# Summing expert answers in DRAM by accumulating scatters instead of storing them apart and adding them later

## The chip, the cores and the metric

The kernel runs on one core of one Trainium2 chip. The metric is the device time in microseconds. The kernel before has a median of 1523.21 us over 3 runs (1523.09 to 1526.4). The profiled execution took 1526.19 us, of which the profile shows a span of 1524.4 us from the first to the last instruction.

## What is computed

The input is four images of 256 channels and 64 x 64 pixels. A first layer (group norm, a 3 x 3 neighbourhood attention, a residual sum) and the attention of a second layer (a gated mean over a window of 64 tokens) come first. Then each of the 16384 tokens, a row of 256 numbers, goes through a mixture of experts:

```python
logits = tokens @ router_w.T
probs = softmax(logits)                    # 8 experts
rw, re = top_k(probs, 2)
rw = rw / maximum(rw.sum(-1), 1e-12)       # two weights that add up to 1
combine = zeros((N, E)).at[arange(N)[:, None], re].set(rw)
out = tokens
for e in range(8):
    h = gelu(tokens @ w1[e] + b1[e]); y = h @ w2[e] + b2[e]
    out = out + combine[:, e:e + 1] * y
x = from_tokens(t + out)                   # back to channels first
```

Only the two chosen experts of a token have a weight that is not zero, so a token needs two answers: 2 x 16384 answers in all.

## The kernel before

Three loops follow one another, each ended by a barrier of all engines.

**Loop 1** runs over 32 blocks of 512 tokens. Besides the first layer and the attention it normalizes each token (tile `tn`), finds the logits and sorts the tokens by expert. Each of a token's two copies goes to the next free row of its expert in the DRAM tensor `sent`, by indirect DMAs of GpSimd (128 rows each, eight for a block, line 1492). A row has 258 numbers: 256 of the token, the row in `answers` where the first copy's answer belongs, and the first expert's number. The residual row of each token, `tt`, is stored in DRAM as `residual`. `power` on GpSimd (line 1484) finds the reciprocal roots of the norms, ahead of the sends. Behind the last block VectorE builds the tables that say which tile belongs to which expert, splits the weights of the experts into two parts for exact products (`lower_parts`), and computes the two weights of every token (`mix`, lines 1450 to 1468) out of the kept logits, with one exponential on ScalarE.

**Loop 2** runs over 72 tiles of 512 sorted rows; 64 would do if every expert's count were a multiple of 512, and the rest are tiles of padding. It is a pipeline in which every engine runs an order that is written out by hand, with stages a fixed number of iterations apart (`LAG`): L loads a tile of rows (`xin`, SyncE), X turns it on TensorE and splits it (`xh` on ScalarE, `xl` on VectorE), H is the first product with its gelu (`hid`, `hh` on ScalarE, `hl` on VectorE), Y is the second product, whose bias VectorE adds into `yy` (line 1770). `yy` has three slots (`YB`). GpSimd then sends the tile's rows to `answers`, each to a place of its own, in four indirect DMAs of 128 rows of 1 KB (line 1627). They wait for `yy` and for the row numbers (`dest_i`), and not for earlier scatters. VectorE waits for a scatter only when it wants to fill the slot that this scatter read, three tiles later.

**Loop 3** runs over 32 blocks of 512 tokens: SyncE loads the two answers of each token (`got`, 1 MB) and the residual (`res`, 0.5 MB); VectorE multiplies and adds (lines 1827 and 1835); TensorE turns the sum to channels first (line 1850); ScalarE copies it out of PSUM (`fin`, two slots) and stores it (0.5 MB).

Of the kernel before, what the change touches and what calls it, by code (L numbers as in the profile page):

```python
# [88 lines left out]
def hybrid(nc, x, wqT, wkT, wvT, wo, bq, bk, bv, bo, wpT, bp, wg, rwT, w1, b1, w2, b2, out):  # L89
    f32 = mybir.dt.float32  # L90
    f32r = mybir.dt.float32r
    bf16 = mybir.dt.bfloat16
    i32 = mybir.dt.int32
# [27 lines left out]
    NJ = 2 * NT // BT + E  # L121
    NJ += NJ % 2
# [7 lines left out]
    with ctx:  # L130
# [9 lines left out]
        residual_v = nc.dram_tensor("residual", [NB, P, KT * C], f32).ap()  # L140

        sent = nc.dram_tensor("sent", [ROOM, C + 2], f32).ap()

        blanks = nc.dram_tensor("blanks", [E * BT, C + 2], f32).ap()

        answers = nc.dram_tensor("answers", [2 * NT + 2 * (E + SPARE) * BT, C], f32).ap()
# [8 lines left out]
        halves = sb("halves", [P, 2, 4])  # L155
        expert_ids = sb("expert_ids", [P, E])
# [35 lines left out]
        tail_id = sb("tail_id", [P, E + SPARE, KT, 2])  # L192
        mix = sb("mix", [P, NB * KT, 2])
# [110 lines left out]
        with nc.Block() as block:  # L304
# [20 lines left out]
            def _(eng):  # L325
# [9 lines left out]
                eng.wait_ge(pool_const, done)  # L335
                eng.memset(ones[:, :], 1.0).then_inc(pool_const, 1)
# [12 lines left out]
                eng.iota(places[:, :], pattern=[[2 * BT, NB], [2, KT]], base=0, channel_multiplier=2 * KT,  # L349
# [69 lines left out]
            def _(eng):  # L419
# [16 lines left out]
                eng.wait_ge(pool_const, 22)  # L436
# [22 lines left out]
            def _(eng):  # L459
# [6 lines left out]
                eng.wait_ge(pool_const, 22)  # L466
# [30 lines left out]
        def lb(name, shape, dt=f32):  # L497
# [33 lines left out]
        tn = lb("tn", [P, 2, KT, C + 2])  # L531
        tnT = lb("tnT", [P, CC, BT])
        logit = lb("logit", [P, KT, E])
        best = lb("best", [P, NB * KT, 8])
# [8 lines left out]

        jvec = lb("jvec", [P, NJ])
        count = lb("count", [P, E])
# [8 lines left out]
        NR = NB * KT  # L554
        fall = tnT[:, :, :].rearrange("p a b -> p (a b)")[:, 0:NR * 8].rearrange("p (r e) -> p r e", e=8)
        spare_f = xn1T[:, :, :].rearrange("p a b -> p (a b)")
        zsum = spare_f[:, 0:NR].rearrange("p (r e) -> p r e", e=1)
        psum2 = spare_f[:, NR:2 * NR].rearrange("p (r e) -> p r e", e=1)
        p12 = spare_f[:, 2 * NR:4 * NR].rearrange("p (r e) -> p r e", e=2)
        sharing = sem("sharing")  # L560
# [40 lines left out]
        route = sig("route", "Ewhere Ebase Eprod Eslotf Esl Dbest Dbesti Didf Dhot DM "  # L601
                             "")
        main_ready = sig("main_ready", "Nmain")
# [63 lines left out]
        with nc.Block() as block:  # L667
            @block.sync
            def _(eng):
                eng.wait_ge(prepared, 1)  # L670

                def body(it):
# [20 lines left out]
                    if it.base is None and it.off == 3:  # L693

                        eng.wait_ge(zeroed, 2)
                        eng.wait_ge(tailed, 1)
# [1213 lines left out]
```

## Time and profile before

| what | before |
|---|---|
| median of 3 runs | 1523.21 us (1523.09 to 1526.4) |
| profiled execution | 1526.19 us, span 1524.4 us |
| PE busy | 1311.8 us (86%) |
| DVE busy | 1065.8 us (70%) |
| ACT busy | 994.5 us (65%) |
| POOL busy | 703.8 us (46%) |
| the 288 scatters to `answers` | 303.7 us of POOL, 1055 ns each |
| bytes by DMA | 252.29 MB, mean 166 GB/s |

The shares are means over three loops with different limits, so they say little by themselves. The page's row of 40 slices shows the loops: TensorE is at nine tenths through loops 1 and 2 with a dip between them, and in the last four slices TensorE falls to two to four tenths while the DMA engines stand at nine tenths and move about 420 GB/s. PE, DVE, ACT, POOL and SP are TensorE, VectorE, ScalarE, GpSimd and SyncE.

### The profile page before, as it was taken

What the parts mean: (1) busy time and instruction counts of PE and PEld (TensorE: products, weight loads), DVE (VectorE), ACT (ScalarE), POOL (GpSimd) and SP (SyncE); (2) the same over time, 40 slices, a digit from 0 to 9 for tenths busy, and PEclk for the clock granted to TensorE, in tenths of its full rate; (3) what the DMA queues carried; (4) which work ended last, traced back from release to release, by engine and by line L of the source; (5) the groups of instructions that cost most, each with busy time, mean ns of one, the idle gap of its engine ahead of it and who ended that gap; (6) DMA issues with size and microseconds to landing.
All of it is one profiled execution on the core that took longest, in us unless ns stands there. A gap on an engine that the chain in (4) does not pass through costs nothing. (4 is left out here: it accounts for less than half of the span.)

```text
span 1524.4 us, 29139 instructions
## 1 busy us (share of the span) xinstructions
PE 1311.8 (86%) x8812; PEld 1151.4 (76%) x8812; DVE 1065.8 (70%) x3724; ACT 994.5 (65%) x2124; POOL 703.8 (46%) x774
## 2 busy tenths in 40 slices
PE   3899999999999999999995199999999999924343
PEld 3788888888888888888875189999999999923232
DVE  5488888888888777877865666555555666537665
ACT  1678788887888778887764177776666667612222
POOL 3115554555545554454443346666666666620000
PEclk9999999999999999999996599999999999965555
DMA  7534554645543222231221655555555555449998
GB/s 276 187 91 116 146 143 119 174 109 153 142 137 109 95 95 91 88 107 66 74 81 57 230 176 164 162 162 162 165 165 168 164 167 167 154 171 420 421 420 331
DMA packets 118072, 252.29 MB, mean 166 GB/s; under 512 B 40608, under 2 KB 54176, under 8 KB 113568
## 3 DMA queue, kind: packets, MB, share of 16 engines
q1 hardware_dynamic: 82976, 159.94, 32.7%
q0 software_dynamic: 26112, 71.60, 13.2%
q10 hardware_dynamic: 8832, 18.89, 3.3%
q8 instruction: 75, 1.23, 0.3%
q14 instruction: 77, 0.63, 0.1%
HBM read 136.80 MB, written 117.80 MB: 167 GB/s over the span
## 5 line engine op out<-in xcount | busy, mean ns | idle before, releaser
L1627 POOL DMA_INDIRECT answers<-yy,dest_i x288 | 303.7, 1055 | 189.1 <-DVE dest_i L1741 116.9
L1492 POOL DMA_INDIRECT sent<-tn,slot_s x256 | 275.7, 1077 | 222.2 <-DVE slot_s L1315 150.0
L1753 DVE TENSOR_TENSOR xl<-m_bank,xh 128x512 fp32r<-128x512 f32 x144 | 93.0, 687 | 180.3 <-ACT xh L1723 180.2
L1717 ACT ACTIVATE hid<-m_bank,b1s 128x512 f32<-128x512 f32 x144 | 99.0, 689 | 135.6 <-issue 87.8
L1676 PE MATMUL s_bank<-band,hh 128*128 x576 | 166.9, 290 | 0.9 <-DVE yy L1770 0.9
L1850 PE MATMUL m_bank<-ident,tot 128*128 128x128 f32 x256 | 62.2, 424 | 117.3 <-ACT fin L1864 85.5
L1676 PE MATMUL s_bank<-band,hl 128*128 x576 | 160.7, 279 | 0.0
L1676 PE MATMUL s_bank<-w_s,hh 128*128 x576 | 160.6, 279 | 0.0
L1850 PEld LDWEIGHTS m_bank<-ident,tot 128*128 128x128 f32 x256 | 50.2, 223 | 129.1 <-issue 70.3
L738 PE MATMUL m_bank<-wvo,band 128*128 128x258 f32 x792 | 133.2, 304 | 13.2 <-DVE band L1300 10.8
L770 PE MATMUL o_bank<-vv,at 128*128 128x256 f32 x512 | 140.0, 396 | 1.3 <-DVE tt L1211 0.7
L1484 POOL TENSOR_TENSOR rs<-ve,halves 128x4 f32<-128x4 f32 x64 | 64.8, 1018 | 153.7 <-DVE ve L1160 153.7
L1864 ACT ACTIVATE fin<-m_bank 128x512 f32<-128x512 f32 x64 | 35.3, 595 | 149.8 <-DMA out_x<-fin 110.1
L738 PEld LDWEIGHTS m_bank<-wvo,band 128*128 128x128 f32 x792 | 107.3, 192 | 29.2 <-issue 27.5
L738 PE MATMUL s_bank<-band,rT 128*128 128x256 f32 x768 | 122.9, 296 | 0.0
L1659 PE MATMUL m_bank<-xh,w1hs 128*128 128x512 f32 x288 | 114.5, 398 | 0.0
L1659 PE MATMUL m_bank<-xh,w1ls 128*128 128x512 f32 x288 | 113.3, 394 | 0.0
L1659 PE MATMUL m_bank<-xl,w1hs 128*128 128x512 f32 x288 | 113.2, 393 | 0.0
L1676 PEld LDWEIGHTS s_bank<-band,hh 128*128 128x128 f32 x576 | 108.5, 188 | 1.2 <-issue 1.1
L1676 PEld LDWEIGHTS s_bank<-w_s,hh 128*128 128x128 f32 x576 | 108.5, 188 | 0.1
L1676 PEld LDWEIGHTS s_bank<-band,hl 128*128 128x128 f32 x576 | 108.3, 188 | 0.0
L738 PEld LDWEIGHTS s_bank<-band,rT 128*128 128x128 f32 x768 | 101.8, 189 | 1.7
(211 smaller groups left out, 3549.1 us busy)
## 6 DMA issues: line engine op xcount, KB each, us to landing
xin<-sent SPq DMA_DIRECT2D x72, 516.0 KB, 3.8
got<-answers SPq DMA_DIRECT2D x32, 1024.0 KB, 8.2
xs<-in_x SPq DMA_DIRECT2D x32, 512.0 KB, 5.6
raw<-in_x SPq DMA_DIRECT2D x32, 512.0 KB
residual<-tt SPq DMA_DIRECT2D x32, 512.0 KB, 2.9
res<-residual SPq DMA_DIRECT2D x32, 512.0 KB, 9.8
out_x<-fin ACTq DMA_DIRECT2D x32, 512.0 KB, 8.7
answers<-yy,dest_i POOLq DMA_INDIRECT x288, 3.3
```

What stands on the lines that cost most here:

```text
L738: last = eng.matmul(dst, lhs(i, c), rhs(j, c), start=(n == 0), stop=(n == len(passes) - 1))
L770: last = eng.matmul(o_bank[:, 0:C], at[:, k % 2, j, :], vv[:, value_slot(it.block("B"), k + j), 0:C], start=(j == 0), stop=(j == 1))
L1484: eng.tensor_tensor(rs[:, n, :], ve[:, n, :], halves[:, 0, 0:KT], ALU.pow).then_inc(root.sem, 1)
L1492: eng.indirect_dma_start(sent, bass.IndirectOffsetOnAxis(slot_s[:, par, j, k:k + 1], 0), tn[:, par, k, :], None).then_inc(scattered[par], 16)
L1627: eng.indirect_dma_start(answers, bass.IndirectOffsetOnAxis(dest_i[:, slot, k:k + 1], 0), yy[:, slot, k, :], None).then_inc(rows_out[slot] ...
L1659: last = eng.matmul(h_bank[f][:, :], w[:, par, c, fs], xx[:, par, c, :], start=(n == 0), stop=(n == 3 * CC - 1))
L1676: last = eng.matmul(y_bank[half][:, k * C:(k + 1) * C], hx[:, par, f, ts], rhs, start=(n == 0), stop=(n == 3 * CC - 1))
L1717: eng.activation(hid[:, f, :], h_bank[f][:, :], ACT.Gelu, bias=b1s[:, par, f:f + 1])\
L1753: eng.tensor_tensor(xl[:, par, c, :], xT_bank[c][:, :], xh[:, par, c, :].bitcast(f32), ALU.subtract).then_inc(xl_ready[c].sem, 1)
L1850: last = eng.transpose(m_bank[c][:, k * P:(k + 1) * P], tot[:, par, k, c * P:(c + 1) * P], ident[:, :])
L1864: eng.activation(fin[:, par, c, :], m_bank[c][:, :], ACT.Copy).then_inc(f_taken[c].sem, 1)
```

## The change

`answers`, `residual` and `mix` go. A tensor `sums` in DRAM, one row of 256 numbers for each token and two blocks of rows for padding, takes the residual rows in loop 1. The two weights are computed in loop 1, block by block: VectorE subtracts the best logit from the second (`fall`), ScalarE takes the exponential (`fell`), and GpSimd makes 1/(1+x) and (1-x)/(1+x) of it (`row_tails`) and writes them with the row number behind the token, so a row in `sent` has 260 numbers. In loop 2 a tile's rows are multiplied by their weights (`pick`), two of the four parts on VectorE and two on ScalarE, and GpSimd adds them to `sums` by indirect DMAs with `compute_op=ALU.add`, in a new stage Z one iteration behind Y. Two tiles may hold the same token, so a tile's scatter waits until the scatter of the tile ahead has landed. Loop 2 has 71 tiles. Loop 3 only loads `sums`, turns it and stores it, with six slots for loads and four for stores.

```diff
-    NJ = 2 * NT // BT + E
-    NJ += NJ % 2
+    NJ = 2 * NT // BT + E - 1
...
+                def fallen(it):
+                    route.wait(eng, it, "Dfall")
+                    tailed_rows.wait(eng, it.before(), "Em")
+                    eng.activation(fell[:, it.parity("D"), :], fall[:, :], ACT.Exp).then_inc(share.sem, 1)
...
+                def row_tails(it):
+                    pe, blk = it.parity("E"), it.block("E")
+                    share.wait(eng, it.before(), "De")
+                    if blk >= 2:
+                        eng.wait_ge(scattered[pe], it.pair("E") * (32 * KT))
+                    eng.tensor_copy(tn[:, pe, :, C], places[:, blk * KT:blk * KT + KT])
+                    eng.tensor_scalar(less[:, :], fell[:, pe, :], 1.0, -1.0, ALU.mult, ALU.add)
+                    eng.tensor_scalar(more[:, :], fell[:, pe, :], 1.0, 1.0, ALU.mult, ALU.add).then_inc(tailed_rows.sem, 1)
+                    tailed_rows.wait(eng, it, "Em")
+                    eng.tensor_tensor(tn[:, pe, :, C + 2], more[:, :], wholes[:, 0, 0:KT], ALU.pow).then_inc(tailed_rows.sem, 1)
+                    tailed_rows.wait(eng, it, "Ep")
+                    eng.tensor_tensor(tn[:, pe, :, C + 3], less[:, :], tn[:, pe, :, C + 2], ALU.mult).then_inc(tailed_rows.sem, 1)
...
-                eng.wait_ge(sharing, 2)
-                eng.reduce_sum(zsum[:, :, 0], fall[:, :, :], AX.X).then_inc(sharing, 1)
...
-                eng.tensor_tensor(mix[:, :, :], p12[:, :, :], psum2[:, :, :].broadcast_to([P, NR, 2]), ALU.mult)
...
-                    if it.runs("Y"):
-
-                        slot = it.block("Y") % YB
-                        alone(eng, (dest_int.sem, dest_int.count(it, "Yd")),
-                              *((y.sem, y.count(it, f"Yt{i}")) for i, y in enumerate(y_taken)))
+                    if it.runs("Z"):
+                        at_ = it.block("Z")
+                        slot = at_ % YB
+                        if at_ > 0:
+                            eng.wait_ge(rows_out[(at_ - 1) % YB], ((at_ - 1) // YB + 1) * 16 * KT)
+                        alone(eng, (scaled_d.sem, scaled_d.count(it.before(), "Ys")), (scaled_a.sem, scaled_a.count(it, "Zs")))
                         for k in range(KT):
                             eng.indirect_dma_start(
-                                answers, bass.IndirectOffsetOnAxis(dest_i[:, slot, k:k + 1], 0),
-                                yy[:, slot, k, :], None).then_inc(rows_out[slot], 16)
+                                sums, bass.IndirectOffsetOnAxis(dest_i[:, at_ % RING, k:k + 1], 0),
+                                yy[:, slot, k, :], None, compute_op=ALU.add).then_inc(rows_out[slot], 16)
...
+                    if it.runs("Z"):
+                        slot, at_ = it.block("Z") % YB, it.block("Z") % RING
+                        y_taken[1].wait(eng, it.before(), "Yt1")
+                        for k in range(2, KT):
+                            last = eng.activation(yy[:, slot, k, :], yy[:, slot, k, :], ACT.Copy, scale=pick[:, at_, k:k + 1])
+                        last.then_inc(scaled_a.sem, 1)
...
+                        y_taken[0].wait(eng, it, "Yt0")
+                        for k in range(2):
+                            last = eng.tensor_scalar(yy[:, slot, k, :], yy[:, slot, k, :],
+                                                     pick[:, it.block("Y") % RING, k:k + 1], None, ALU.mult)
+                        last.then_inc(scaled_d.sem, 1)
...
+        GOT, FIN = 6, 4
+        got = cb("got", [P, GOT, KT, C])
+        fin = cb("fin", [P, FIN, CC, BT])
...
+                        if blk >= GOT:
+                            user = Iteration(None, blk - GOT, NB)
+                            alone(eng, (f_full[0].sem, f_full[0].count(user, "Kf0")),
+                                  (f_full[1].sem, f_full[1].count(user, "Kf1")))
+                        eng.dma_start(got[:, blk % GOT, :, :].rearrange(flat), sums_of(blk)).then_inc(got_in[blk % GOT], 16)
```

On GpSimd, at the end of loop 1 and the start of loop 2, this stands before; the names in brackets are the semaphores that an instruction waits for, and `rows_out0` to `rows_out2` are raised when a scatter of that slot has landed:

```order
L1492 DMA sent<-tn,slot_s 139264x258 [waits route]
L1492 DMA sent<-tn,slot_s 139264x258 x7
L667 UNCONDITIONAL_BRANCH [waits scattered1,scattered0]
L1618 UNCONDITIONAL_BRANCH [waits barrier_Pool_Activation_PE_DVE_SP_gather]
L1627 DMA answers<-yy,dest_i 49152x256 [waits y_taken1,dest_int,y_taken0]
L1627 DMA answers<-yy,dest_i 49152x256 x3
```

And this stands there now:

```order
L1490 TENSOR_TENSOR tn<-more,wholes 128x4 [waits tailed_rows]
L1492 TENSOR_TENSOR tn<-less,tn 128x4 [waits tailed_rows]
L1500 DMA sent<-tn,slot_s 138752x260 [waits route,tailed_rows]
L1500 DMA sent<-tn,slot_s 138752x260 x7
L671 UNCONDITIONAL_BRANCH [waits scattered1,scattered0]
L1620 UNCONDITIONAL_BRANCH [waits barrier_Pool_Activation_PE_DVE_SP_gather]
L1630 DMA sums<-yy,dest_i 17408x256 [waits scaled_d,scaled_a]
L1630 DMA sums<-yy,dest_i 17408x256 x3
L1630 DMA sums<-yy,dest_i 17408x256 [waits scaled_a,rows_out0,scaled_d]
L1630 DMA sums<-yy,dest_i 17408x256 x3
```

The first scatter of each tile now also waits for the landing of the tile ahead, and nothing else stands on this queue in loop 2.

On VectorE, one tile of loop 2 before:

```order
L1741 CAST dest_i<-dest 128x4 [waits dest_ready,rows_out2]
L1748 SCALAR_TENSOR_TENSOR dest<-xin,expert_f 128x4 [waits dest_int,rows_in2]
L1753 TENSOR_TENSOR xl<-m_bank,xh 128x512 [waits xh_ready0]
L1753 TENSOR_TENSOR xl<-m_bank,xh 128x512 [waits xh_ready1]
L1758 TENSOR_TENSOR hl<-hid,hh 128x512 [waits hh_ready0]
L1758 TENSOR_TENSOR hl<-hid,hh 128x512 [waits hh_ready1]
L1588 TENSOR_LOAD expert_i
L1588 ISA x2
L1770 ISA [waits y_full0,rows_out2]
L1770 TENSOR_TENSOR yy<-s_bank,b_all 128x512
L1770 TENSOR_TENSOR yy<-s_bank,b_all 128x512 [waits y_full1]
```

And now:

```order
L1748 SCALAR_TENSOR_TENSOR pick<-xin,expert_f 128x4 [waits rows_in2]
L1751 CAST dest_i<-xin 128x4
L1753 TENSOR_TENSOR pick<-pick,xin 128x4 [waits dest_ready]
L1757 TENSOR_TENSOR xl<-m_bank,xh 128x512 [waits xh_ready0]
L1757 TENSOR_TENSOR xl<-m_bank,xh 128x512 [waits xh_ready1]
L1762 TENSOR_TENSOR hl<-hid,hh 128x512 [waits hh_ready0]
L1762 TENSOR_TENSOR hl<-hid,hh 128x512 [waits hh_ready1]
L1774 ISA [waits y_full0,rows_out2]
L1774 TENSOR_TENSOR yy<-s_bank,b_all 128x512
L1774 TENSOR_TENSOR yy<-s_bank,b_all 128x512 [waits y_full1]
L1780 TENSOR_SCALAR yy<-yy,pick 128x256 [waits y_taken0]
L1780 TENSOR_SCALAR yy<-yy,pick 128x256
```

Two multiplications of `yy` and one small sum are new, and the wait for the slot's earlier scatter stays on the bias sum.

## Rows read from the trace of the kernel before

**Rows 1.** Busy time by stretch: bounds, length, engines (instructions), PEclk, DMA share, GB/s.

```profile
35.00:820.00 785.00, 755.82 (x5268) 652.03 (x5268) 618.05 (x2703) 613.42 (x1369) 371.60 (x439) 0.98 0.38 116
890.00:1340.00 450.00, 449.14 (x3068) 409.80 (x3067) 270.86 (x554) 311.38 (x619) 296.94 (x281) 1.00 0.51 163
1357.00:1524.40 167.40, 62.21 (x256) 50.17 (x256) 112.50 (x288) 35.29 (x64) 0.00 (x0) 0.50 0.97 392
```

**Rows 2.** The scatters of 62 tiles of loop 2: duration, first and last start; landing.

```profile
L1627 POOL DMA_INDIRECT answers<-yy,dest_i x248: 954/961/1429, 908.4 to 1306.0; - x124
...
DMA to landing us min/median/max: 2.4/3.5/4.6
```

**Rows 3.** Timeline of one tile of loop 2: start, length, instruction, idle before it.

```profile
1095.64 0.96 POOL L1627 DMA_INDIRECT answers<-yy,dest_i  x1 [1.25 <-DVE dest_i L1741]
...
1097.86 1.16 ACT L1728 ACTIVATE hh<-hid 128x512 fp32r<-128x512 f32 x2
...
1098.73 1.29 DVE L1758 TENSOR_TENSOR hl<-hid,hh 128x512 fp32r<-128x512 f32 x2
...
1099.44 1.41 POOL L1627 DMA_INDIRECT answers<-yy,dest_i  x1 [0.30 <-issue]
...
1101.13 0.16 DVE L1741 CAST dest_i<-dest 128x4 int32<-128x4 f32 x1
...
1102.10 0.96 POOL L1627 DMA_INDIRECT answers<-yy,dest_i  x1 [1.25 <-DVE dest_i L1741]
```

**Rows 4.** First scatter of a tile, the one that starts at 1102.1: its landing.

```profile
DMA to landing us min/median/max: 2.4/2.4/2.4
```

**Rows 5.** Fourth scatter of the same tile, in the same way.

```profile
L1627 POOL DMA_INDIRECT answers<-yy,dest_i x1: 1410/1410/1410, 1105.9 to 1105.9; - x1
...
DMA to landing us min/median/max: 3.0/3.0/3.0
```

**Rows 6.** DMA issues of the whole span: size, median us from issue to landing.

```profile
xin<-sent SPq DMA_DIRECT2D x72, 516.0 KB, 3.8
...
wg_s<-in_wg SPq DMA_DIRECT2D x1, 0.5 KB, 2.0
```

**Rows 7.** Groups between 200 and 800 us, shapes apart: busy us, mean ns.

```profile
L1040 ACT ACTIVATE tt<-tt,sum_bias,sum_scale 128x256 f32<-128x256 f32 x100 | 51.9, 607 | 0.0
...
L1174 DVE TENSOR_SCALAR tn<-tt,mv,rs 128x256 f32<-128x256 f32 x100 | 34.5, 408 | 0.0
```

**Rows 8.** Waits of loop 2 (890 to 1340 us): total us, times, longest.

```profile
ACT hid L1717 <- issue: 87.8, 68, 1.6
```

**Rows 9.** All scatters of loop 2: duration, first and last start.

```profile
L1627 POOL DMA_INDIRECT answers<-yy,dest_i x288: 954/961/1455, 890.3 to 1348.0; - x144
```

**Rows 10.** Timeline of GpSimd in one block of loop 1.

```profile
712.58 2.03 POOL L1484 TENSOR_TENSOR rs<-ve,halves 128x4 f32<-128x4 f32 x2 [5.16 <-DVE ve L1160]
719.57 1.07 POOL L1492 DMA_INDIRECT sent<-tn,slot_s  x1 [4.96 <-DVE slot_s L1315]
```

**Rows 11.** Timeline between loops 1 and 2.

```profile
855.15 0.96 POOL L1492 DMA_INDIRECT sent<-tn,slot_s  x1 [0.30 <-issue]
...
857.60 1.21 DVE L1455 TENSOR_REDUCE xn1T<-tnT 128x128 f32<-128x1024 f32 x1
...
861.86 0.43 DVE L1468 TENSOR_TENSOR mix<-xn1T 128x256 f32<-128x256 f32 x1
```

**Rows 12.** Timeline between loops 2 and 3.

```profile
1347.97 0.96 POOL L1627 DMA_INDIRECT answers<-yy,dest_i  x1 [0.30 <-issue]
...
1369.12 1.97 PE L1850 MATMUL m_bank<-ident,tot 128*128 128x128 f32 x8 [1.86 <-DVE tot L1835]
```

**Rows 13.** Loop 3 (1357 to 1524 us): GB/s in 40 slices, and packets.

```profile
GB/s 259 424 329 356 412 424 417 418 426 419 413 434 407 423 416 422 434 411 411 421 423 425 425 413 421 415 421 421 420 430 416 413 424 421 426 410 391 149 251 126
DMA packets 17495, 65.62 MB, mean 393 GB/s; under 512 B 1488, under 2 KB 1488, under 8 KB 13392
```

**Rows 14.** Busy time by stretch, early in loop 1, columns as in the first group.

```profile
60.00:70.00 10.00, 8.74 (x58) 7.71 (x57) 6.22 (x18) 6.76 (x15) 1.51 (x4) 1.00 1.09 356
```

More of the change, by code:

```diff
@@ L1096, in body @@
                         expo(it, 3)
+                    if d:
+                        fallen(it)
                     if a:
@@ L1734, in body @@
                 def body(it):
-                    if it.runs("Y"):
-                        slot = it.block("Y") % YB
-                        if it.block("Y") >= YB:
-                            eng.wait_ge(rows_out[slot], it.block("Y") // YB * 16 * KT)
-                        dest_ready.wait(eng, it.before().before().before(), "Xd")
-                        eng.tensor_copy(dest_i[:, slot, :], dest[:, it.block("Y") % 4, :]).then_inc(dest_int.sem, 1)
                     if it.runs("X"):
@@ L1818, in body @@
                     if it.runs("K"):
-                        par, at_, slot = it.parity("K"), it.block("K") * KT, it.block("K") % RES
-                        tot_ready.wait(eng, it.before(), "Kt")
-                        share_ready.wait(eng, it.before(), "Ks")
-                        eng.tensor_copy(share[:, :, :], mix[:, bass.ds(at_, KT), :]).then_inc(share_ready.sem, 1)
-                        share_ready.wait(eng, it, "Ks")
-                        eng.wait_ge(res_in[slot], it.block("K") // RES * 16 + 16)
@@ L1825, in body @@
-                        eng.wait_ge(got_in[slot], it.block("K") // RES * 16 + 16)
-                        for k in range(KT):
-                            last = eng.scalar_tensor_tensor(part[:, k, :], got[:, slot, k, 0, :],
-                                                            share[:, k, 0:1], res[:, slot, k, :],
-                                                            ALU.mult, ALU.add)
-                        last.then_inc(part_ready.sem, 1)
-                        part_ready.wait(eng, it, "Kp")
@@ L1832, in body @@
-                        for i in range(CC):
-                            f_full[i].wait(eng, it.before(), f"Kf{i}")
-                        for k in range(KT):
-                            last = eng.scalar_tensor_tensor(tot[:, par, k, :], got[:, slot, k, 1, :],
-                                                            share[:, k, 1:2], part[:, k, :],
-                                                            ALU.mult, ALU.add)
-                        last.then_inc(tot_ready.sem, 1)
-                tiles_loop(eng, NB, body)
@@ L1841, in _ @@
[L1841 to L1852 removed]
+                        blk = it.block("K")
```

196 lines of the change are left out of this document (86 added, 110 removed).

## The prediction, made before the changed kernel was run

> **What bounds the kernel now.** I read the busy time by stretch first. In loop 1 TensorE is busy 755.82 of 785 us, in loop 2 449.14 of 450 us at a granted clock of 1.00; in loop 3 it is busy 62.21 of 167.4 us, and there the DMA engines have a share of 0.97 [rows 1]. So loops 1 and 2 go at TensorE's pace and loop 3 at that of the transfers. Then I read the scatters of loop 2 by their line: between 908.4 and 1306.0 us lie 61 periods of a tile and the three steps from a tile's first scatter to its fourth, so a tile takes (397.6 - 3.8) / 61 = 6.46 us [rows 2]. The timeline of one tile shows what GpSimd does in it: the four scatters start 1.27 us apart, (1099.44 - 1095.64) = 3.80 us from the first to the fourth, and then the engine sits idle for 1.25 us [rows 3]. That idle time costs nothing now, since a scatter waits for no other scatter. Last I asked for single scatters and their landings: the first of a tile landed 2.4 us after its start, the fourth 3.0 us after it, and over the loop the median is 3.5 [rows 2, 4, 5].
>
> **The new wait in loop 2.** This is the term that decides. A tile's first scatter may not start before the fourth of the tile ahead has landed. One turn of that circle is: 3.80 us from first to fourth start; L, the time from the fourth's start to its landing; and the time in which GpSimd wakes and starts. The wake shows in the trace: the last thing that a tile waits for, `dest_i`, ends at 1101.13 + 0.16 = 1101.29, and the scatter starts at 1102.10, 0.81 us later, behind as many waits as it has in the new kernel [rows 3]. So the period is T = 4.61 + L. With the shortest landing of a plain scatter, 2.4, T is 7.0 us, and that is over the 6.46 us of TensorE. So from the rows alone the circle of scatters sets the pace of loop 2, whatever the addition costs. Behind the waiting scatter nothing else stands on GpSimd's queue; who waits for it is VectorE, three tiles later, which wants the slot of `yy`, and through VectorE all of the pipeline.
>
> L is what the trace doesn't show, since no DMA in it adds. From below: a plain scatter, 2.4 us alone and 3.0 us beside VectorE's `hl`, when its own issue took 1.41 us and not 0.96 [rows 3 to 5]. I take 2.7 for it, for the circle will drift past `hl` and the new multiplications. From above: the addition fetches the row from DRAM before it can write, and if that were a whole small load from DRAM in front of the write it would cost 2.0 us [rows 6], so L = 4.7. Between them: 515.5 KB more than half a KB cost a load 3.8 - 2.0 = 1.8 us, so the 128 KB more that an adding scatter reads cost 0.45 us; some of the load's latency comes on top. I take 0.8 us in all, so L = 3.5, nearer to the row on bytes than to the row on a whole load, and T = 8.1 us.
>
> The Trainium skill, "DMA: Bandwidth & Descriptors", section "Anatomy of one DMA - SWDGE (gpsimd) path", says a DMA of GpSimd costs a fixed 2.0 us and its bytes at 436 GB/s. For 128 KB that is 2.3 us, and the trace agrees with 2.4. Taken at its word an adding scatter (256 KB moved) would land in an estimated 2.6 us, T would be 7.2 and the sum below about 1500 us.
>
> **The rest of loop 2.** VectorE gets two multiplications of 128x256, 34.5 / 100 = 0.35 us each, and one small operation of some 0.2 us; ScalarE gets two of 52 / 100 = 0.52 us [rows 7]. ScalarE has 87.8 us of idle time in 68 tiles before `hid`, 1.3 us a tile [rows 8], which takes its 1.04 us in even at the old pace; VectorE is busy 270.86 of 450 us [rows 1]. At T = 8.1 both lie free. If the circle were no limit they would cost nothing either. The first scatter comes later: the multiplications on ScalarE stand behind the next tile's `hh`. At the old pace that is `hh`'s end, 1097.86 + 1.16 = 1099.02 us where the scatter of before starts at 1095.64 [rows 3], plus 1.04 and 0.81, thus 5.2 us later. The first scatter of before starts at 890.3 us [rows 9], so now at about 895.5.
>
> [...]
>
> **Loop 1 and the gap behind it.** GpSimd gets five small operations in a block. The one known is the power, 2.03 / 2 = 1.0 us; the others I take at 0.3 us, so 2.3 us with their waits. They stand where GpSimd is idle for 4.96 us ahead of its sends [rows 10], so they are hidden; without that cover they would cost 32 x 2.3 = 74 us. VectorE and ScalarE change by one small operation a block under a busy TensorE. Behind loop 1 VectorE loses the weights' chain, 857.60 to 862.29. GpSimd's last send starts at 855.15 [rows 11]; with the last block's five operations ahead of it, and landing in traffic some 3 to 4 us later, it ends at about 861. So the barrier is reached about when it was, 0 to 2 us earlier: I take 0.
>
> **The end of loop 2.** One tile fewer is in the sum as 71. The last scatter's start to the first load of loop 3 is 1357.0 - 1348.0 = 9.0 us; without the landing of 2.6, 6.4 us. The scatter is in [rows 12]; the load is where the stretch of loop 3 begins [rows 1]. The landing is the one I take for a plain scatter with no tile being loaded beside it, between 2.4 and 2.7.
>
> **Loop 3.** Before, 65.62 MB moved in 167.4 us, at about 420 GB/s in most slices [rows 13]: 156 us, and 11 us of ends. Now 32 x (0.524 + 0.524) = 33.6 MB make 80 us, 2.5 us a block. TensorE's eight transposes take 1.97 us a block at half clock [rows 12], under that, and VectorE's and ScalarE's copies are 0.6 us. With six loads ahead the ends are shorter: 8 us. So 88 us, 79 less.
>
> **The sum** of the profiled execution: 895.5 + 70 x 8.1 (567) + 3.8 + 3.5 + 6.4 + 88 = 1564.2 us of span, and 1.8 us around it; the median of the runs lies 3.0 us under the profiled execution, so 1563 us. In general it is 1315 + 71 L. Break-even with 1523 is at L = 2.93.
>
> **Rivals.**
> (1) The addition costs nearly nothing: it only moves more bytes, 0.45 us, and the circle misses `hl`. L = 2.4 to 2.85 gives 1485 to 1517 us, faster. For it: the burst of a scatter is short, and a transfer could fetch all of its rows at once. Against it: even 0.1 us above the fourth landing of 3.0 us turns the gain.
> (2) The addition is dear: a whole load in front of the write (L = 4.7) gives 1649 us, and if GpSimd needs longer for its descriptors, all four scatters at 1.41 for 0.96 us, 1.8 us more a tile, up to 1777 us. For it: a descriptor more for each row; against it: nothing in the trace.
> (3) TensorE loses its clock. It would wait 1.6 of 8.1 us. At half clock a tile is nearly 13 us of TensorE; if a third of the tiles ran so, 24 x 4.8 = 115 us more, 1678 us. Against it: at 8.74 us busy in 10 the clock stood at 1.00 [rows 14]; a share of 0.8 isn't in the trace.
> (4) The wait is hidden: it would need a landing under 1.85 us. Then 6.46 x 70 gives about 1447 us. Every landing in the trace is longer.
>
> **How the numbers follow.** Forecast 0.48; (1) 0.26; (2) 0.17; (3) 0.04; (4) 0.02; the rest, a landing just at break-even, 0.03. The range 1492 to 1648 leaves out a tenth on each side: below, most of (4) and the lower end of (1); above, the dear end of (2) and (3). The forecast's own range is 1530 to 1610. Under 0.3% this kernel can't be told from no change. Faster 0.27, same 0.05, slower 0.68.
>
> **What would show it.** GpSimd's scatters start in groups of four with the same distance, 1.27 us, and between groups a gap that ends by a DMA landing and not by VectorE; period 8.1 us. TensorE is busy about 80% of loop 2. Loop 3 takes 88 us. The prediction is wrong if the fourth scatter lands in under 2.9 us, if the distance between scatters grows, or if TensorE's clock drops in loop 2.

## The result, and the profile of the changed kernel

| | before | after |
|---|---|---|
| median of the runs | 1524.81 us (1523.09 to 1526.89, 4 runs) | 1730.84 us (1724.35 to 1731.43, 4 runs) |
| ratio, 95% interval | | 1.1341 [1.1308, 1.1374] |
| span of the profiled execution | 1524.4 us | 1729.4 us |
| first to last scatter of loop 2 | 457.7 us | 743.1 us |
| loop 3, from its first load | 167.4 us | 85.6 us |

The change made the kernel 13.4% slower. The 205 us between the two spans come apart like this: loop 3 gives 81.8 us back, the stretch from the last scatter to the first load of loop 3 gives 0.9, the first scatter comes 2.3 us later, and from the first to the last scatter loop 2 takes 285.4 us more.

The page of the changed kernel first, as far as it speaks of loop 2: engines, the scatters, the transfer of a tile's rows (KB, us from issue to landing), GpSimd's queue, and packets.

```profile
PE 1387.2 (80%) x8768; PEld 1217.8 (70%) x8768; DVE 1029.1 (60%) x3665; ACT 1037.7 (60%) x2256; POOL 920.6 (53%) x931
...
DMA packets 140392, 218.85 MB, mean 127 GB/s; under 512 B 39504, under 2 KB 89936, under 8 KB 139984
...
q0 software_dynamic: 53184, 71.34, 23.2%
...
L1630 POOL DMA_INDIRECT sums<-yy,dest_i x284 | 460.1, 1620 | 319.5 <-DMA sums<-yy,dest_i 197.7
...
xin<-sent SPq DMA_DIRECT2D x71, 520.0 KB, 4.7
```

284 scatters (71 tiles, four each) take 1.62 us of GpSimd each on average, where those of before took 1.06, and 1.56 us in the median, where those of before took 0.96 [rows 9]. The greater part of the idle time ahead of them ends with a landing. The tile's load lands 0.9 us later than before [rows 6].

Busy time by stretch, with the columns of [rows 1]:

```profile
35.00:820.00 785.00, 755.30 (x5272) 650.74 (x5272) 619.93 (x2710) 615.10 (x1399) 426.17 (x587) 0.98 0.37 117
890.00:1620.00 730.00, 541.22 (x3017) 487.88 (x3015) 328.11 (x750) 368.39 (x749) 447.65 (x277) 0.85 0.58 97
1650.00:1729.00 79.00, 46.27 (x244) 39.38 (x242) 21.43 (x31) 18.51 (x31) 0.00 (x0) 0.69 1.02 401
```

Loop 1 is what it was: TensorE is busy 755.30 us for 755.82. In loop 2 nothing is full: TensorE is busy 541.22 of 730 us, GpSimd 447.65, and the DMA engines have a share of 0.58. A stretch in which nothing is full goes in a circle of waits. The waits of that stretch (us in all, times, longest) name it:

```profile
DVE yy L1774 <- DMA sums<-yy,dest_i: 388.1, 67, 9.5
...
POOL sums L1630 <- DMA sums<-yy,dest_i: 194.7, 63, 4.7
...
PE s_bank L1679 <- DVE yy L1774: 172.7, 66, 5.9
```

GpSimd waits for the landing of the tile ahead, VectorE for a slot of `yy` whose scatter hasn't landed, and TensorE for VectorE: the order in which the prediction put them.

Then the timeline of one turn of the circle, as in [rows 3]:

```profile
1104.01 1.56 POOL L1630 DMA_INDIRECT sums<-yy,dest_i  x1 [2.94 <-DMA sums<-yy,dest_i]
...
1105.87 1.56 POOL L1630 DMA_INDIRECT sums<-yy,dest_i  x1 [0.30 <-ACT yy L1737]
1106.04 0.34 SPq L1613 DMA_DIRECT2D xin<-sent  x1
...
1106.86 1.28 DVE L1762 TENSOR_TENSOR hl<-hid,hh 128x512 fp32r<-128x512 f32 x2
...
1107.73 1.85 POOL L1630 DMA_INDIRECT sums<-yy,dest_i  x1 [0.30 <-issue]
...
1109.89 1.56 POOL L1630 DMA_INDIRECT sums<-yy,dest_i  x1 [0.30 <-issue]
...
1114.47 1.56 POOL L1630 DMA_INDIRECT sums<-yy,dest_i  x1 [3.03 <-DMA sums<-yy,dest_i]
```

The starts lie 1.86, 1.86 and 2.16 us apart, 5.88 us from the first to the fourth for 3.80 before. The third is longer because VectorE's `hl` lies beside it, as it lay beside the fourth in [rows 3]. The fourth scatter's landing:

```profile
L1630 POOL DMA_INDIRECT sums<-yy,dest_i x1: 1558/1558/1558, 1109.9 to 1109.9; - x1
...
DMA to landing us min/median/max: 3.8/3.8/3.8
```

So a turn is 5.88 + 3.8 + 0.8 = 10.5 us, and 1114.47 - 1104.01 = 10.46. The 0.8 us from the landing to the next tile's first scatter has a median of 0.79 over the 70 turns and is under 1.0 us in 64 of them, so little else than the landing holds the next tile back. Over the loop the view of the scatters by their line (shortest, median and longest duration in ns; first and last start; landing) says the same:

```profile
L1630 POOL DMA_INDIRECT sums<-yy,dest_i x284: 1557/1560/1853, 892.6 to 1635.7; - x142
...
DMA to landing us min/median/max: 3.7/4.0/5.8
```

(743.1 - 5.6) / 70 = 10.54 us a tile, where the kernel before needed 6.46. The 5.6 are the last tile's three steps (5.88 us in the turn above).

The end, as in [rows 12], and the transfers of loop 3 (1650 us to the end), as in [rows 13]:

```profile
1635.73 1.56 POOL L1630 DMA_INDIRECT sums<-yy,dest_i  x1 [0.30 <-issue]
...
1643.82 1.28 SPq L1814 DMA_DIRECT2D got<-sums  x3
```

```profile
DMA packets 12797, 31.68 MB, mean 399 GB/s; under 512 B 976, under 2 KB 976, under 8 KB 12793
```

Loop 3 is still bound by its transfers (a DMA share of 1.02 in the table of stretches), which are half as many bytes.

### The profile page after: what moved, and what is told of

Same layout as the page of the kernel before. It is cut to its first block and busy times, and to the rows that moved or that the text cites. A ratio compares the mean times of both kernels' runs of the same rounds, so it can differ in the third digit from the quotient of the medians.

```text
span 1729.4 us, 29067 instructions
## 1 busy us (share of the span) xinstructions
PE 1387.2 (80%) x8768; PEld 1217.8 (70%) x8768; DVE 1029.1 (60%) x3665; ACT 1037.7 (60%) x2256; POOL 920.6 (53%) x931
## 3 DMA queue, kind: packets, MB, share of 16 engines
q0 software_dynamic: 53184, 71.34, 23.2%
## 5 line engine op out<-in xcount | busy, mean ns | idle before, releaser
L1630 POOL DMA_INDIRECT sums<-yy,dest_i x284 | 460.1, 1620 | 319.5 <-DMA sums<-yy,dest_i 197.7
L1679 PE MATMUL s_bank<-band,hh 128*128 x568 | 204.5, 360 | 172.7 <-DVE yy L1774 172.7
L1774 DVE TENSOR_TENSOR yy<-s_bank,b_all 128x512 f32<-128x512 f32 x142 | 91.5, 686 | 388.2 <-DMA sums<-yy,dest_i 388.1
L1679 PEld LDWEIGHTS s_bank<-band,hh 128*128 128x128 f32 x568 | 145.7, 257 | 188.6 <-issue 188.5
L1679 PE MATMUL s_bank<-w_s,hh 128*128 x568 | 196.4, 346 | 0.0
L1679 PEld LDWEIGHTS s_bank<-band,hl 128*128 128x128 f32 x568 | 146.4, 258 | 0.0
L1679 PEld LDWEIGHTS s_bank<-w_s,hh 128*128 128x128 f32 x568 | 146.4, 258 | 0.0
L1737 ACT ACTIVATE yy<-yy,pick 128x256 f32<-128x256 f32 x142 | 64.6, 503 | 92.8 <-DVE yy L1774 92.7
L1826 PE MATMUL m_bank<-ident,got 128*128 128x128 f32 x256 | 49.2, 365 | 70.8 <-DMA got<-sums 43.8
L745 PE MATMUL m_bank<-band,wqk 128*128 128x512 f32 x384 | 101.2, 400 | 0.0
```

The source lines that it names most:

```text
L745: last = eng.matmul(dst, lhs(i, c), rhs(j, c), start=(n == 0), stop=(n == len(passes) - 1))
L1630: eng.indirect_dma_start(sums, bass.IndirectOffsetOnAxis(dest_i[:, at_ % RING, k:k + 1], 0), yy[:, slot, k, :], None, compute_op=ALU.add). ...
L1679: last = eng.matmul(y_bank[half][:, k * C:(k + 1) * C], hx[:, par, f, ts], rhs, start=(n == 0), stop=(n == 3 * CC - 1))
L1737: last = eng.activation(yy[:, slot, k, :], yy[:, slot, k, :], ACT.Copy, scale=pick[:, at_, k:k + 1])
L1774: eng.tensor_tensor(yy[:, slot, 2 * half:2 * half + 2, :], y_bank[half][:, :].rearrange("p (k c) -> p k c", k=2), b2_all[:, bass.ds(e, 1), ...
L1826: last = eng.transpose(turned_bank(it, c)[:, k * P:(k + 1) * P], got[:, blk % GOT, k, c * P:(c + 1) * P], ident[:, :])
```

## The experiments

The theory (A): loop 2 goes in a circle of issue, landing and wake; the addition makes GpSimd's issue of each scatter longer, and the landing too. The rival (B) puts the time into the DMA engines: the adding scatters crowd them and land late, the longer issues only fill time that would be waited anyway, and fewer or smaller scatters shorten the landing as well. The first four kernels separate the addition from the wait. The last eight ran on another chip of the same kind, on which the kernel before takes 1617 to 1655 us instead of 1521, so each is compared only with the kernel before on its own chip. The changed kernel itself was not run on that chip. The first scatter of the kernels with adding scatters starts at 941.6 to 948.9 us there, where it started at 892.6 here, so their times are some 50 us longer before loop 2 has begun, and neither they nor their ratios can be set beside 1731 us or 1.134. What is compared for them is the period.

### The wait without the addition

```diff
-                                yy[:, slot, k, :], None, compute_op=ALU.add).then_inc(rows_out[slot], 16)
+                                yy[:, slot, k, :], None).then_inc(rows_out[slot], 16)
```

> The changed kernel with plain scatters in the place of adding ones; the wait for the tile ahead stays. What is left out: the answers overwrite the rows of sums and aren't added. Theory A (the adding makes both the issue and the landing of a scatter longer: 1.56 for 0.96 us and 3.8 for 2.5 us): the starts come 1.27 us apart again, the fourth lands in 2.4 to 2.9 us, the period of a tile falls from 10.5 to about 7.2 us, and the time to about 1500 us. Theory B (the issue is longer because of something else in the new loop, the multiplications beside it or the longer rows, and not because of the adding): the starts stay 1.87 us apart, the period is about 9.3 us, and the time about 1645 us.

Measured: 1521.28 us against 1520.99, ratio 0.9997 [0.9968, 1.0026]. Its scatters:

```profile
L1630 POOL DMA_INDIRECT sums<-yy,dest_i x284: 954/960/1480, 891.7 to 1425.4; - x142
...
DMA to landing us min/median/max: 2.4/3.1/4.6
```

Without the addition the issue is 0.96 us again. The fourth scatter of a tile lands after 2.7 us (median), so the sum of the prediction for a plain scatter, 4.61 + 2.7 = 7.31, is met by the median period of 7.31 us. The mean is 7.57, since in some tiles a landing or an issue is longer, and that is why the time is over the 1500 of theory A. So a plain scatter with the wait just eats up what loop 3 gives, and what lies between this kernel and the changed one is the addition, with nothing else different.

### The addition without the wait

The tiles take turns in four tensors, so that none needs to wait; the four aren't summed.

```diff
+        others = [nc.dram_tensor(f"others{i}", [NT + 2 * BT, C], f32).ap() for i in range(4)]
...
-                        if at_ > 0:
-                            eng.wait_ge(rows_out[(at_ - 1) % YB], ((at_ - 1) // YB + 1) * 16 * KT)
...
-                                sums, bass.IndirectOffsetOnAxis(dest_i[:, at_ % RING, k:k + 1], 0),
+                                others[at_ % 4], bass.IndirectOffsetOnAxis(dest_i[:, at_ % RING, k:k + 1], 0),
```

> The changed kernel with its adding scatters spread over four tensors in turn, so that a tile needn't wait for the tile ahead (the tensor's last use lies four tiles back, which VectorE has waited for). What is left out: the answers are missing from the result. Theory A (the period is three issues + landing + wake; without the wait the four issues alone are left): GpSimd issues without a break, 4 x 1.87 and about 0.3 us beside hl, period 7.5 to 7.8 us, still over TensorE's 6.46, and a time of about 1525 us. Theory B (the DMA engines take the adding rows no faster than about one tile in 10 us): the landings grow and the period stays near 10 us, about 1700 us.

Measured: 1530.49 us, ratio 1.0069 [1.0046, 1.0092], as theory A said (about 1525). Scatters, and the stretch of loop 2:

```profile
L1629 POOL DMA_INDIRECT others<-yy,dest_i x284: 1557/1562/2082, 892.4 to 1436.8; - x142
```

```profile
890.00:1430.00 540.00, 457.30 (x3015) 406.25 (x3013) 315.21 (x750) 364.20 (x749) 452.53 (x280) 0.98 0.79 132
```

GpSimd's issues alone are now the limit: four steps of 1.87 us are 7.5 us and the period is 7.70. The longer issue is there without the wait, so it isn't an effect of the wait. The DMA engines' share rises to 0.79, from 0.58 in the changed kernel, so they can take the same adding scatters faster and weren't what bound it. TensorE's clock stays near full speed (0.98).

### Neither wait nor addition

The kernel above without `compute_op`.

```diff
-                                yy[:, slot, k, :], None, compute_op=ALU.add).then_inc(rows_out[slot], 16)
+                                yy[:, slot, k, :], None).then_inc(rows_out[slot], 16)
```

> As the run with four tensors, with plain scatters: neither adding nor the wait for the tile ahead. What is left out: the answers are missing from the result. If all that the changed kernel loses comes from these two, the period falls back to TensorE's 6.46 us, TensorE's clock stays at 1.00 in the loop, and the time is 1315 - 8 + 71 x 1.85, about 1445 us. If the multiplications on VectorE and ScalarE, now at the old pace, cost something of their own, the period is 6.6 to 7 us and the time 1455 to 1485 us.

Measured: 1431.57 us, ratio 0.9413 [0.937, 0.9456].

```profile
L1629 POOL DMA_INDIRECT others<-yy,dest_i x284: 954/960/1214, 889.0 to 1332.8; - x142
```

```profile
890.00:1330.00 440.00, 431.52 (x2993) 395.14 (x2991) 320.33 (x744) 358.55 (x742) 269.03 (x280) 1.00 0.50 161
```

TensorE sets the pace again (431.52 of 440 us, clock 1.00), at 6.29 us a tile. The new weights, multiplications and the stage Z are therefore free, as forecast. The time is 13 us under the 1445 expected, for the period is 6.35 us in the median where 6.46 was taken; no run shows why it is shorter than in the kernel before. The four kernels, all against the same runs of before:

| | no wait | wait for the tile ahead |
|---|---|---|
| plain scatter | 1431.6 us | 1521.3 us (+90) |
| adding scatter | 1530.5 us (+99) | about 1725 us (+293) |

(The last is 1.1341 x 1521.) The two costs don't add: 90 + 99 is 189, and both together cost 293. Without the wait, the issues compete with TensorE and the longer of the two counts, so of four steps of 1.87 us only what lies over 6.3 us is paid. With the wait, the longer issues, the longer landing and the wake follow each other and every part is paid.

### The kernel before with the wait

`at_` is the tile's number; nothing else is changed.

```diff
-                        slot = it.block("Y") % YB
+                        slot, at_ = it.block("Y") % YB, it.block("Y")
+                        if at_ > 0:
+                            eng.wait_ge(rows_out[(at_ - 1) % YB], ((at_ - 1) // YB + 1) * 16 * KT)
```

> The kernel before with one thing added: a tile's first scatter waits for the landing of the tile ahead. Its scatters are plain and its result is the full one. The period by the terms of the prediction is 3.8 + 2.4 to 2.9 + 0.8, so 7.0 to 7.5 us in the place of 6.46, and with 72 tiles the time is 1565 to 1600 us. If a plain scatter's wait were hidden by TensorE's pace, the time would stay at 1524.

Measured: 1622.26 us, ratio 1.0667 [1.0636, 1.0698]. This misses the upper end of the expectation by 22 us. Two scatters, a cast on VectorE and the next tile's first scatter, from its timeline:

```profile
1052.11 0.96 POOL L1629 DMA_INDIRECT answers<-yy,dest_i  x1 [2.24 <-DVE dest_i L1743]
...
1053.37 1.50 POOL L1629 DMA_INDIRECT answers<-yy,dest_i  x1 [0.31 <-issue]
...
1058.87 0.17 DVE L1743 CAST dest_i<-dest 128x4 int32<-128x4 f32 x1 [3.64 <-DMA answers<-yy,dest_i]
...
1059.65 0.96 POOL L1629 DMA_INDIRECT answers<-yy,dest_i  x1 [2.25 <-DVE dest_i L1743]
```

The period is 7.54 us (1059.65 - 1052.11, also the median; the mean is 7.72). 0.5 us of it lies in the second scatter, 1.5 us where 0.96 was counted; the rest, 3.2 us of landing and wake behind the fourth, is a little under the 3.5 of the plain chain. So the wait alone slows this kernel too, without any addition; the kernel before differs in nothing else. The view puts the idle time down to `dest_i`, but the landing ends it: the cast had itself waited 3.64 us for a landing, and GpSimd starts 0.61 us behind the cast's end, where a scatter that `dest_i` released started 0.81 us behind it [rows 3].

### Three and two scatters of a tile instead of four

```diff
-                        for k in range(KT):
+                        for k in range(3):
```

(and `range(2)` in the second; the waits count as many.) If the circle is issue, landing and wake, each scatter left out takes one step of the issue away.

> The changed kernel with three adding scatters for a tile in the place of four. What is left out: a quarter of the answers. Theory A (a period is the issues in a row, then one landing of 3.8 us and a wake of 0.8 us, whatever the number of scatters): one issue less, the period falls by 1.87 us from 10.5 to 8.6 us, the time to about 1600 us. Theory B (the landing of the last is so long because the scatters ahead of it are still being worked off): the landing shrinks too, to 3 us or less, the period is under 8 us and the time under 1560 us.

> The same with two scatters for a tile; half of the answers are left out. Theory A: 1.87 + 3.8 + 0.8 = 6.5 us, and 0.3 more where hl stretches one of them, so just at or above TensorE's pace of 6.35 us; time 1445 to 1470 us. Theory B: the circle would take under 5.5 us, TensorE alone sets the pace, and GpSimd waits for the other engines and not for a landing; time about 1435 us.

Measured: with three 1674.34 us against 1624.17, ratio 1.0308 [1.0264, 1.0352]; with two 1593.78 us, ratio 0.9812 [0.9641, 0.9984], an interval so wide (two executions, 1582.39 and 1605.17 us) that only the period says anything.

```profile
L1630 POOL DMA_INDIRECT sums<-yy,dest_i x213: 1556/1562/2048, 946.3 to 1575.6; - x107
...
DMA to landing us min/median/max: 3.7/4.4/5.6
```

```profile
1100.89 1.56 POOL L1630 DMA_INDIRECT sums<-yy,dest_i  x1 [4.55 <-DMA sums<-yy,dest_i]
1102.76 1.56 POOL L1630 DMA_INDIRECT sums<-yy,dest_i  x1 [0.30 <-ACT yy L1737]
1102.93 8.73 SPq L1613 DMA_DIRECT2D xin<-sent  x2
...
1109.28 1.56 POOL L1630 DMA_INDIRECT sums<-yy,dest_i  x1 [4.97 <-DMA sums<-yy,dest_i]
```

and the second scatter of this tile:

```profile
L1630 POOL DMA_INDIRECT sums<-yy,dest_i x1: 1558/1558/1558, 1102.8 to 1102.8; - x1
...
DMA to landing us min/median/max: 5.7/5.7/5.7
```

The periods are 8.94 and 8.0 us (median of the second 8.28), longer than either theory said (8.6 or under 8; 6.5 to 6.8 or TensorE's pace). The landing isn't one number. With three scatters the median landings are 3.83, 5.47 and 4.41 us by place; with two, 3.86 and 5.56. The third's gives 3.73 + 4.41 + 0.8 = 8.94, the second's 1.87 + 5.56 + 0.8 = 8.23. With the landing that each kernel shows the circle closes again, to 0.05 us of the medians. Theory B, by which fewer scatters land sooner, falls: the last one's landing went from 3.8 to 4.4 and 5.6 us. In each of the three kernels it is the second scatter that lands late, and each time SyncE issues the 520 KB load of a tile's rows beside it (1102.93 here, 1106.04 in the changed kernel). With four scatters the last is behind that load and lands after 3.8 us. So the circle holds and the constant landing in the expectation did not. The trace of the changed kernel tells the load from the place: 62 scatters have a load issued between 0.5 us before their start and 1.5 us behind it, 57 second ones but also four first ones and a fourth, and all 62 land after 5.2 to 5.8 us; the other 70 fourth ones land after 3.8 us (median; the longest 4.8). No kernel was run with the load moved.

### Half rows

```diff
+        halfs = nc.dram_tensor("halfs", [NT + 2 * BT, C // 2], f32).ap()
...
-                                yy[:, slot, k, :], None, compute_op=ALU.add).then_inc(rows_out[slot], 16)
+                                yy[:, slot, k, 0:C // 2], None, compute_op=ALU.add).then_inc(rows_out[slot], 16)
```

> The changed kernel with adding scatters of half a row each (512 bytes), 128 rows each as before, to a tensor of their own. What is left out: the answers are missing from the result. Theory A (the longer issue goes by rows, the work of writing descriptors, and the longer landing by the fetch from DRAM, neither by bytes): issue stays at 1.56 us, landing falls by no more than 0.4 us, period 10.0 to 10.4 us, time 1700 to 1725 us. Theory B (both go by bytes): issue toward 1.26 us or less and landing toward 3.1, period 9 us or less, time under 1630 us.

Measured: 1746.41 us against 1624.17, ratio 1.0752 [1.0702, 1.0802].

```profile
L1631 POOL DMA_INDIRECT halfs<-yy,dest_i x284: 1558/1561/2102, 941.6 to 1649.5; - x142
```

Half the bytes, the same 1.56 us: the issue costs by row and not by byte. The period is 9.97 us (median), at the edge of theory A's 10.0 to 10.4 and far from B's 9, and 0.5 less than 10.48, and as the steps are unchanged the landing must be about 9.97 - 5.88 - 0.8 = 3.3 us; this trace has no landings of its own for these scatters. So most of the landing is by row or fixed, too: 64 KB less in each direction save half a microsecond of 3.8.

### Toward a faster kernel

Two things of the change are worth having without its addition: 71 tiles in place of 72, and less traffic in loop 3. First the tile alone:

```diff
-    NJ = 2 * NT // BT + E
-    NJ += NJ % 2
+    NJ = 2 * NT // BT + E - 1
```

> The kernel before with 71 tiles in loop 2 and nothing else of the change; full result. Expected: one period of 6.46 us less, so 0.4% faster than before, 1515 us where before is at 1521. If the tiles of padding at the end were hidden behind something, no difference.

Measured: 1648.28 us against 1654.66, ratio 0.995 [0.9928, 0.9972], about one period of a tile.

Then the residual rows of loop 3, of which seven blocks instead of three are now fetched while loop 2 still runs:

```diff
-        RES = 3
+        RES, GOT = 7, 3
```

> The kernel before with 71 tiles and seven blocks of the residual loaded ahead of loop 3 in the place of three; full result. Loop 3 goes at the pace of its transfers, 2.1 MB a block at 420 GB/s, so four blocks of 0.5 MB less in it should give 5 us, with the tile 11 to 12 us in all: 0.75% faster. If loop 3 were bound by the circle of its stores (two slots of fin, which the chain of waits shows) rather than by bytes, only the tile's 6.5 us come.

Measured: 1645.03 us, ratio 0.9924 [0.989, 0.9959], not told apart from the tile alone. Loop 3 still takes 167.4 us. Its stretch and the wait in it that comes first:

```profile
1480.00:1647.00 167.00, 62.28 (x256) 50.19 (x256) 112.36 (x287) 35.39 (x64) 0.00 (x0) 0.50 0.95 380
```

```profile
ACT fin L1865 <- DMA out_x<-fin: 107.3, 26, 8.0
```

ScalarE waits for one of two slots of `fin`, whose store must have landed: perhaps a circle again, in which fewer bytes don't matter; the runs with four slots below test this. Next the answers in bf16 (16 bits; they are rounded once more than in the other kernels, and the result is that of the reference only to that rounding), which halves the bytes of `got`. This kernel also loads eight blocks of the residual ahead, not seven:

```diff
-        answers = nc.dram_tensor("answers", [2 * NT + 2 * (E + SPARE) * BT, C], f32).ap()
+        answers = nc.dram_tensor("answers", [2 * NT + 2 * (E + SPARE) * BT, C], bf16).ap()
...
-        yy = eb("yy", [P, YB, KT, C])
+        yy = eb("yy", [P, YB, KT, C], bf16)
...
-        got = cb("got", [P, GOT, KT, 2, C])
+        got = cb("got", [P, GOT, KT, 2, C], bf16)
```

> As the run with more residual loaded ahead (eight blocks), and the answers are stored in DRAM and loaded as bf16, half the bytes; the two are still multiplied and added to the residual in fp32, so the result has the rounding of the answers to bf16 in it. Loop 3 then moves 1.57 MB a block in the place of 2.1 MB, 50.3 MB less 4.2 MB loaded ahead: 110 us at 420 GB/s and about 11 us of ends in the place of 167, so 46 us less, and with the tile about 53 us: 1468 us, 3.5% faster. If instead VectorE's eight operations a block (8 x 0.42 = 3.3 us, 3.5 with the small ones) or the store's circle set the pace, loop 3 takes 4 to 5 us a block, 130 to 160 us, and the time is 1480 to 1510 us.

Measured: 1629.08 us, ratio 0.9844 [0.9812, 0.9877], 1.6% and not the 3.5% expected. Loop 3 takes 143.4 us and not the 121 that the bytes would give; the same wait is still there:

```profile
ACT fin L1865 <- DMA out_x<-fin: 77.3, 24, 5.1
```

So four slots for the stores, with bf16 answers and, as a kernel of its own, with fp32 ones:

```diff
-        fin = cb("fin", [P, 2, CC, BT])
+        FIN = 4
+        fin = cb("fin", [P, FIN, CC, BT])
```

> As the run with bf16 answers, with four slots for stores in loop 3 in the place of two. Theory A (with two slots the circle copy, store, slot free set the pace of loop 3 once the bytes were fewer, 143 us where the bytes ask for 110): with four slots VectorE sets it, 8 x 0.42 + 0.17 = 3.5 us a block, so 112 us and 11 of ends, 20 us less than with two slots, and 3 to 3.5% faster than before on the same chip. Theory B (the transfers themselves are slower in this mix): loop 3 stays at 140 to 145 us and the gain at 1.6%.

> As the run with seven blocks of residual loaded ahead, all in fp32, with four slots for stores in the place of two; full result. If the store's circle was what took the gain of the residual loaded ahead, loop 3 goes from 167 to 158 us or less. If the transfers set the pace by their bytes, four blocks of residual are already away and it would be 162, the same as the bytes said for two slots, where 167 was measured; anything near 167 says that the bytes loaded ahead didn't come out of loop 3's time at all.

Measured: with bf16 1576.06 us against 1617.16, ratio 0.9752 [0.9709, 0.9795]; with fp32 1608.11 us, ratio 0.9935 [0.9907, 0.9963]. Loop 3 of the first and of the second:

```profile
1440.00:1571.00 131.00, 63.03 (x256) 50.23 (x256) 112.31 (x287) 38.21 (x64) 0.00 (x0) 0.50 0.91 353
```

```profile
1442.00:1604.00 162.00, 62.98 (x256) 50.19 (x256) 112.38 (x287) 38.22 (x64) 0.00 (x0) 0.50 0.97 392
```

The wait for a slot of `fin` is gone in both. The bf16 one is 2.5% faster than the kernel before on its chip, where 3 to 3.5% were expected. VectorE, with 112.31 of 131 us, is what comes next in it, and 132.0 us were measured for the 123 expected. With fp32 answers the wider ring gives loop 3 only 5 us (162.4 for 167.4), which is what the four blocks loaded ahead are worth at 420 GB/s. There the DMA engines have a share of 0.97, and VectorE waits for `got`:

```profile
DVE part L1829 <- DMA got<-answers: 39.8, 25, 4.7
```

These 5 us are read from the traces; the times of the two fp32 kernels, 0.9935 and 0.9924 of before, don't tell them apart.

## Why the prediction was wrong in size

The direction and the mechanism were right: slower, by the circle of GpSimd's scatters. The span came out 165.2 us over the sum of 1564.2 us. By its own terms:

| term | forecast | measured | us |
|---|---|---|---|
| first scatter | 895.5 | 892.6 | -2.9 |
| 70 periods | 8.1 | 10.54 | +170.5 |
| last tile's three steps | 3.8 | 5.6 | +1.8 |
| its landing and the start of loop 3 | 9.9 | 8.1 | -1.8 |
| loop 3 | 88 | 85.6 | -2.4 |

By its last paragraph the prediction was to be wrong if the fourth scatter landed in under 2.9 us, if the distance between scatters grew, or if TensorE's clock dropped in loop 2. The second and the third came about.

- **The step that failed is the start of the circle, "3.80 us from first to fourth start".** It was read from scatters that don't add and taken for the new ones without a reason. The issue of an adding scatter takes 1.56 us for 0.96, and with its 0.3 us behind it a step is 1.87 for 1.27, 5.88 us for three with `hl` beside one of them. That is 2.1 of the 2.44 us by which the period was missed, 146 of 170 us. The plain scatter with the wait confirms the rest of the sum (median period 7.31 us, as the sum says), and the adding scatter without it shows the longer issue by itself.
- **L was sized nearly right:** 3.8 us for the 3.5 taken, inside the bounds of 2.7 and 4.7; 0.3 us a tile, 21 us in all. Taken against the plain scatter's 2.7 the addition costs 1.1 us of landing, not the 0.8, and against the 2.4 of plain scatters that no load crosses 1.4.
- **The bounds were set for the landing alone.** For the issue the prediction had only "against it: nothing in the trace", inside the rival that the addition is dear, and left it out of the range. But the trace said nothing of it in either direction. The row that would have bounded it was there: 1.41 us beside `hl` [rows 3], and that rival's own sum with all four at 1.41, and L = 3.8 in place of 4.7, is a span of 1564 + 71 x 0.3 + 71 x 1.8 = 1713 us (1729.4 measured). That rival, with 0.17, had named the longer issue; its size was beyond the 1.41 too.
- **Rival 1, the addition nearly free,** with a landing under 2.85, fell: no landing of an adding scatter is under 3.7 us. The estimate of 2.6 us from the Trainium skill, "DMA: Bandwidth & Descriptors", section "Anatomy of one DMA - SWDGE (gpsimd) path", goes with it. The trace disagrees (3.8 us); without the addition the formula's 2.3 us stand beside 2.4 measured.
- **Rival 3, TensorE's clock, came true without its price.** In four windows of the turn shown above (PE, PEld, DVE, ACT, POOL, then granted clock, DMA share, GB/s):

```profile
1104.00:1106.00 2.00, 1.72 (x11) 1.72 (x12) 2.00 (x8) 1.37 (x4) 1.69 (x2) 0.81 0.00 0
1106.00:1108.00 2.00, 2.00 (x11) 2.00 (x11) 2.00 (x4) 0.71 (x3) 1.70 (x2) 0.50 0.99 115
1108.00:1110.00 2.00, 2.00 (x11) 1.80 (x11) 0.15 (x1) 0.00 (x0) 1.70 (x2) 0.84 0.87 240
...
1112.00:1114.50 2.50, 0.48 (x5) 0.24 (x3) 0.69 (x2) 2.34 (x5) 0.03 (x1) 1.00 0.47 52
```

  TensorE waits some 2 us at the end of a turn, starts, falls to 1.2 GHz (0.50) for a few microseconds and is back at 2.4 GHz (1.00) before it runs dry again. It waits 172.7 us for VectorE all the same, and GpSimd, which closes the circle, waits for landings, so a faster clock would only have lengthened that wait. This is argued from the waits; no run changed the clock alone.
- **Right as forecast:** the weights of loop 1, the new multiplications, the moved start of loop 2, and loop 3. The five small operations of GpSimd take 1.9 us a block where 2.3 were taken, and lie in its idle time; loop 1's TensorE time is unchanged. The power is 1.07 of them, from the groups of 200 to 800 us:

```profile
L1490 POOL TENSOR_TENSOR tn<-more,wholes 128x4 f32<-128x4 f32 x25 | 26.7, 1068 | 2.1
L1492 POOL TENSOR_TENSOR tn<-less,tn 128x4 f32<-128x4 f32 x25 | 6.0, 240 | 2.0
```

- **The longer scatter beside `hl`** came again. Of the 284 adding scatters 58 took over 1.70 us, and all 58 lie beside `hl`; the 67 that lie beside a new multiplication and not beside `hl` took 1.56 us in the median and none over 1.67. The Trainium skill, "SBUF - State Buffer", section "Who interferes with whom", says that a VectorE instruction with two inputs in SBUF contends with a GpSimd instruction that reads SBUF, and infers that a `tensor_tensor` leaves the writing of descriptors alone. `hl` is a `tensor_tensor` with two inputs in SBUF, and the trace agrees that it holds GpSimd up (1.85 for 1.56 us in the turn above); no run here shows which part of the scatter it is that waits.

## What to carry to other kernels

When a wait closes a circle, every part of it is paid in full each turn, also parts that were free before: price each of them for the new instruction (the time on its engine, the landing, the wake) and not only the one that the change is about. "Nothing in the trace" bounds nothing, so an operation's own time on the engine that issues it belongs in the range. Here an accumulating scatter that orders each tile behind the last cost more than the traffic that it saved; keeping the rows independent, with a narrower type and enough slots for the stores, made the kernel 2.5% faster instead.

## What the runs showed of the hardware

- An indirect DMA that adds holds GpSimd for 1.56 us per 128 rows and one that doesn't for 0.96; it is by rows, since rows of 512 bytes cost the same as rows of 1024. A plain scatter of 128 rows makes 48 packets on GpSimd's queue and an adding one 144. This is worked out from 53184 packets in the changed kernel and 25920 in the same kernel with plain scatters, 96 more for each of 284 scatters; 25920 / (256 + 284) is 48. With half rows it is 53184 again. The plain kernel's row, for the one of the changed kernel above:

```profile
q0 software_dynamic: 25920, 71.34, 13.0%
```

- Its landing, with no load of a tile beside it, is 3.8 us for 2.4; 3.3 with half rows (worked out from the period).
- A small scatter that is issued just ahead of a 520 KB load lands after 5.2 to 5.8 us, and the one behind it after 4.4 (a plain one 4.4 and 3.6 in the kernel before); a circle with few scatters feels it, one with four doesn't.
- The same program took 1521 us on one chip and 1617 to 1655 us on another, where its median differed by 2% from one set of runs to the next. The 71-tile kernel has loop 1 longer there, at a lower granted clock (0.94, with 792.88 us of TensorE in 900, for 0.98 [rows 1]), and its tile takes 7.07 us on average for 6.46 (scatters from 975.6 to 1474.1 us). Its 512 KB loads of the input land after 8.8 us for 5.6. What makes it so isn't in these traces. The window of its loop 1, columns as above:

```profile
35.00:935.00 900.00, 792.88 (x5340) 681.58 (x5340) 634.25 (x2792) 626.83 (x1396) 382.41 (x453) 0.94 0.35 104
```

- A store of 512 KB takes 8.7 us to land in loop 3 of the changed kernel; two slots made such stores the limit of the kernels with less traffic, four removed that wait.
